# A Mamba-2 mixer with an FFN on one core: the state update as three passes of split operands, and one buffer for gated values

## What is computed

```python
proj = x @ in_proj_w.T                       # gate 8192 | hs 8192, B 1024, C 1024 | dt 128
hBC = silu(causal_conv4(proj[hs, B, C]))     # 4 taps per channel
xch = hs * dt                                # per head (128 heads of 64, 8 groups of B and C with 128 states)
# chunks of 128 tokens, 4 in a batch, A_cum = cumsum(dt * A) inside a chunk
Y_diag = (C @ B.T * exp(segsum)) @ xch
states = einsum('lhn,hl,lhp->hpn', B, exp(A_cum[-1] - A_cum), xch)   # what a chunk adds to the state
state  = state * exp(A_cum[-1]) + states                             # carried to the next chunk
Y_off  = (C @ state) * exp(A_cum)
g = (Y_diag + Y_off + hs * D) * silu(gate)
out = rmsnorm_per_group(g) * norm_w @ out_proj_w.T
x = layernorm(x + out);  x = layernorm(x + x @ W.T + bias + lora(x))
```

## Time and profile before

| | |
|---|---|
| median of 3 runs | 1648.08 us (1647.91 to 1648.45) |
| the profiled execution's own time | 1651.37 us |
| its span in the profile | 1648.4 us |
| PE busy | 1614.3 us, 98% of the span |
| DVE, ACT, POOL busy | 1348.8 us, 1221.5 us, 1021.2 us |
| granted TensorE clock, mean | 0.996 of 2.4 GHz |
| DMA | 178.65 MB, 33.7% of 16 engines on the main queue |

### The profile page before, as it was taken

One profiled execution on the slowest core, in us unless ns is written; L12 is line 12 of the kernel. 1 busy time (PEld: TensorE's weight loads), 2 busy tenths in 40 slices (PEclk: granted clock), 3 DMA queues, 4 the chain that ended last, 5 costly groups with the idle time before them and its releaser, 6 DMA issues. The chain is left out here.

```text
span 1648.4 us, 26983 instructions
## 1 busy us (share of the span) xinstructions
PE 1614.3 (98%) x9072; PEld 1292.7 (78%) x9072; DVE 1348.8 (82%) x1855; ACT 1221.5 (74%) x2373; POOL 1021.2 (62%) x829
## 2 busy tenths in 40 slices
PE   7999999999999999999999999999999999999898
PEld 6777888778888788878887788887887878877655
DVE  5677798869987799877988689986998879887876
ACT  5868778776777877776787777788677778777742
POOL 4456667566675757656665656756566666666654
PEclk9999999999999999999999999999999999999999
DMA  3633324333242333423243333433323332333301
GB/s 125 238 110 103 113 84 157 88 103 103 84 158 84 113 96 107 132 91 113 92 123 118 99 100 94 145 97 113 99 100 120 103 119 94 108 110 102 128 27 45
DMA packets 87144, 178.65 MB, mean 108 GB/s; under 512 B 16480, under 2 KB 20576, under 8 KB 86624
## 3 DMA queue, kind: packets, MB, share of 16 engines
q1 hardware_dynamic: 83760, 175.72, 33.7%
q10 hardware_dynamic: 3248, 1.22, 0.3%
HBM read 172.17 MB, written 4.72 MB: 107 GB/s over the span
## 5 line engine op out<-in xcount | busy, mean ns | idle before, releaser
L952 POOL TENSOR_TENSOR w_lo<-raw,w_hi 128x512 fp32r<-128x512 f32 x209 | 297.9, 1426 | 295.5 <-ACT w_hi L709 294.5
L495 PE MATMUL proj<-x_hi,w_hi 128*128 128x512 f32 x1160 | 462.8, 399 | 8.5 <-DVE x_lo L1216 6.9
L496 PE MATMUL proj<-x_lo,w_hi 128*128 128x512 f32 x1160 | 452.9, 390 | 0.0
L497 PE MATMUL proj<-x_hi,w_lo 128*128 128x512 f32 x1160 | 452.8, 390 | 0.0
L1103 DVE SCALAR_TENSOR_TENSOR hs<-proj,uch,hs 128x511 f32<-128x511 f32 (+2 forms) x384 | 285.4, 744 | 56.9 <-ACT hs L736 51.6
L791 ACT ACTIVATE decay<-decay,tok 128x128 f32<-128x128 f32 x1024 | 312.5, 392 | 0.0
L1004 POOL TENSOR_TENSOR dh<-dh,eac 128x512 f32<-128x512 f32 x96 | 127.8, 1331 | 228.5 <-DVE eac L1151 228.4
L495 PEld LDWEIGHTS proj<-x_hi,w_hi 128*128 128x128 f32 x1160 | 218.9, 189 | 50.8 <-issue 6.9
L1125 DVE TENSOR_TENSOR decay<-decay,cb 128x1024 f32<-128x1024 f32 x128 | 190.9, 1491 | 80.2 <-ACT decay L797 77.7
L497 PEld LDWEIGHTS proj<-x_hi,w_lo 128*128 128x128 f32 x1160 | 218.3, 188 | 46.0
L496 PEld LDWEIGHTS proj<-x_lo,w_hi 128*128 128x128 f32 x1160 | 219.0, 189 | 41.6
(11 more groups left out here) (121 smaller groups left out, 2765.7 us busy)
## 6 DMA issues: line engine op xcount, KB each, us to landing
decay<-acum_d SPq DMA_DIRECT2D x128, 512.0 KB, 4.0
raw<-w_t SPq DMA_DIRECT2D x209, 256.0 KB, 2.8
eac<-eacum_d SPq DMA_DIRECT2D x192, 128.0 KB, 4.1
wo_raw<-wo_t SPq DMA_DIRECT2D x32, 256.0 KB, 3.6
c_new<-wo_t SPq DMA_DIRECT2D x32, 256.0 KB, 4.8
hs<-x_t SPq DMA_DIRECT2D x8, 256.0 KB, 5.3
acc<-x_tok SPq DMA_DIRECT2D x1, 2048.0 KB, 8.6
out<-acc SPq DMA_DIRECT2D x8, 256.0 KB, 2.0
```

The costliest lines, as they stand in the source:

```text
L495: nc.tensor.matmul(dst[:], w_hi[:, ws, k, :], x_hi[:, k, cols], start=(k == 0), stop=False)
L496: nc.tensor.matmul(dst[:], w_hi[:, ws, k, :], x_lo[:, k, cols], start=False, stop=False)
L497: mm = nc.tensor.matmul(dst[:], w_lo[:, ws, k, :], x_hi[:, k, cols], start=False, stop=(k == KC - 1))
L952: nc.gpsimd.tensor_tensor(w_lo[:, s].rearrange("p a b -> p (a b)"), raw[:, s, :], w_hi[:, s].rearrange("p a b -> p (a b)").bitcast(F32), A ...
```

## The change

Four things move together.

1. The state update becomes three F32R matmuls, b_hi·xd_hi, b_hi·xd_lo and b_lo·xd_hi. B in token order is stored as `b_hi` and `b_lo` for the six chunks of a group that update a state (VectorE: one copy and one subtraction in the place of one copy; for chunks 3 and 7 no transpose and no copy at all). GpSimd makes `xd`, then casts it to `xd_hi` and subtracts to `xd_lo`, with a wait for its own result between them.
2. On TensorE the update comes behind `front` instead of ahead of it. VectorE's `front` therefore waits for `xd_scaled`, GpSimd's last reading of `xdt`.
3. `g_hi` and `g_lo` have one buffer. `g_hi` waits for `out_ready` of the step before (`s`, not `s - 1`). ScalarE makes the square first and `g_hi` after it; VectorE makes `g_lo` after the sums of squares and the layer norms' statistics.
4. `eac` has one buffer; its load waits for `dh_ready` of the step before its use and stands first in the step's list on SyncE.

```diff
 def load_eac(q, g, e, c):
-            slot = (carried(0, e, c) - 1) % 2
-            wait(q, dh_ready, step(g, e, c) - 1)
+            wait(q, dh_ready, step(g, e, c))
...
                         mm.then_inc(yd_ready, 1)
+                        off, ne, ncn = after(e, c)
+                        if not (last and off):
+                            front(g + off, ne, ncn)
                         if c % CPB != CPB - 1:
                             pe.wait_ge(xd_ready, updates(g, e, c))
                             wait(pe, yoff_scaled, carried(g, e, c))
-                            nc.tensor.matmul(p_st[:], b_tok[:, c, :], xd[:].rearrange("p a b -> p (a b)"),
-                                             start=True, stop=True).then_inc(st_ready, 1)
-                        off, ne, ncn = after(e, c)
-                        if not (last and off):
-                            front(g + off, ne, ncn)
+                            xh, xl = xd_hi[:].rearrange("p a b -> p (a b)"), xd_lo[:].rearrange("p a b -> p (a b)")
+                            nc.tensor.matmul(p_st[:], b_hi[:, bslot(c), :], xh, start=True, stop=False)
+                            nc.tensor.matmul(p_st[:], b_hi[:, bslot(c), :], xl, start=False, stop=False)
+                            nc.tensor.matmul(p_st[:], b_lo[:, bslot(c), :], xh, start=False, stop=True).then_inc(st_ready, 1)
...
                         act.wait_ge(gated, s + 1)
-                        wait(act, out_ready, s - 1)
-                        nc.scalar.activation(g_hi[:, c % 2].rearrange("p a b -> p (a b)"), y[:].rearrange("p a b -> p (a b)"),
-                                             ACT.Copy).then_inc(ghi_ready, 1)
                         wait(act, sqs_ready, s)
                         nc.scalar.activation(ysq[:], y[:], ACT.Square).then_inc(sq_ready, 1)
+                        wait(act, out_ready, s)
+                        nc.scalar.activation(g_hi[:].rearrange("p a b -> p (a b)"), y[:].rearrange("p a b -> p (a b)"),
+                                             ACT.Copy).then_inc(ghi_ready, 1)
...
-                nc.gpsimd.tensor_tensor(xd[:], xdt[:], bcast(tok[:, e, 2, c, :], 2, HD), ALU.mult).then_inc(xd_ready, 1)
+                n = updates(g, e, c)
+                nc.gpsimd.tensor_tensor(xd[:], xdt[:], bcast(tok[:, e, 2, c, :], 2, HD), ALU.mult).then_inc(xd_scaled, 1)
+                pool.wait_ge(xd_scaled, n)
+                nc.gpsimd.tensor_copy(xd_hi[:], xd[:]).then_inc(xdhi_ready, 1)
+                pool.wait_ge(xdhi_ready, n)
+                nc.gpsimd.tensor_tensor(xd_lo[:], xd[:], xd_hi[:].bitcast(F32), ALU.subtract).then_inc(xd_ready, 1)
...
                 dve.wait_ge(hid_ready, step(g, e, c) + 1)
+                wait(dve, xd_scaled, carried(g, e, c))
                 nc.vector.tensor_tensor(xdt[:], p_hid[:], bcast(tok[:, e, 1, c, :], 2, HD), ALU.mult).then_inc(xdt_ready, 1)
...
-                        dve.wait_ge(ghi_ready, s + 1)
-                        nc.vector.tensor_tensor(g_lo[:, c % 2].rearrange("p a b -> p (a b)"), y[:].rearrange("p a b -> p (a b)"),
-                                                g_hi[:, c % 2].rearrange("p a b -> p (a b)").bitcast(F32), ALU.subtract).then_inc(glo_ready, 1)
-                        if c < 7 and (c + 1) % CPB and len(STEP_TILES[e][c]) == 1:
-                            scale_off(g, e, c + 1)
                         for ln in lns:
                             ln_stats_1(*ln)
                         dve.wait_ge(sq_ready, s + 1)
...
                         for ln in lns:
                             ln_stats_3(*ln)
+                        dve.wait_ge(ghi_ready, s + 1)
+                        nc.vector.tensor_tensor(g_lo[:].rearrange("p a b -> p (a b)"), y[:].rearrange("p a b -> p (a b)"),
+                                                g_hi[:].rearrange("p a b -> p (a b)").bitcast(F32), ALU.subtract).then_inc(glo_ready, 1)
+                        if c < 7 and (c + 1) % CPB and len(STEP_TILES[e][c]) == 1:
+                            scale_off(g, e, c + 1)
```

More of the change, by code:

```diff
@@ L131, in mixer_ffn_kernel @@
         ysq = sb("ysq", [P, UT, P])
-        g_hi, g_lo = sb("g_hi", [P, 2, UT, P], F32R), sb("g_lo", [P, 2, UT, P], F32R)
+        g_hi, g_lo = sb("g_hi", [P, UT, P], F32R), sb("g_lo", [P, UT, P], F32R)
         state = sb("state", [P, UH, HD])
@@ L449, in body @@
                     for c in range(8):
+                        o1, e1, c1 = ahead(e, c, 1)
+                        if c1 % CPB and not (last and o1):
+                            load_eac(sp, g + o1, e1, c1)
                         od, ed, cd = ahead(e, c, 2 if c % 2 else 4)
@@ L452, in body @@
                             load_decay(sp, g + od, ed, cd)
-                        o2, e2, c2 = ahead(e, c, 2)
-                        if c2 % CPB and not (last and o2):
-                            load_eac(sp, g + o2, e2, c2)
                         for t in tiles_of(e, c, last):
```

47 lines of the change are left out of this document (28 added, 19 removed).

## The result

The changed kernel takes 1665.51 us (median of 4 runs, 1662.74 to 1666.32), the kernel before 1648.22 (4 runs, 1647.91 to 1648.45): a ratio of 1.0102, with a 95% interval of 1.0085 to 1.012. That is 17.3 us slower, where 4.7 were forecast and the range ended at 1664. The profiled execution took 1662.74 us, its span 1660.9.

What follows compares the result with a forecast made beforehand. TensorE alone was taken to set the time up to about 1550 us; −21.8 + 2.5 + 3.4 + 6.4 + 13.7 + 2.5 − 2 = +4.7 us on the 1648.08 median gave 1652.8 us, range 1642 to 1664.

Steps and rivals of the forecast that it cites:

- the price of GpSimd's contention: GpSimd's new cast and subtraction slow VectorE: +6.4 us in (0, 1) and +2.5 us in (1, 4).
- +6.4 us for (0, 1): Step (0, 1): new GpSimd work slows one g_lo in VectorE's unbroken run, 0.8 us in each of 8 groups.
- +2.5 for (1, 4): Step (1, 4): TensorE waits 0.35 us for the state in seven groups; bounds 0 to 7 us.
- GpSimd's work blocking VectorE whole: Rival: each new operation costs 2.0 us, not 0.8, in (0, 1); +9.6 us, 1662.4 us; chance 0.18.
- grown to 1.4: Sign in the profile: the wait ahead of project_out in (0, 1) grows from 0.2 to about 1.4 us.
- a rival of 0.07 behind tile C: Rival: the clock falls at each wait for tile C, 3.1 us seven times; +22 us, 1675 us; chance 0.07.
- the last unit's term: Last unit: earlier statistics save 5.8 us, waits at lora_down cost 3.9; net −2 us, bounds −6 to +6.
- The update and the transposes, −21.8: TensorE: shorter updates save 20.2 us and 16 dropped transposes of B 1.6 us; bounds −18 to −25.
- Gains lost ahead of hs, +2.5: Step (0, 7): transposes wait for ScalarE's silus, so 0.31 us of savings is lost in each of 8 groups.
- Lost ahead of `wo_lo`, +3.4: Step (0, 1): project_out waits for VectorE's wo_lo, so 0.42 us of savings is lost in each of 8 groups.
- Tile C, +13.7: Step (1, 1): g_hi's one buffer delays tile C's weight split; TensorE waits 1.95 us in seven groups.
- `eac`, 0: The one-buffer load of eac takes 4 us, needed a step of 11 us later; cost nothing.

Runs made afterwards that it cites:

- e3: Changed kernel without GpSimd's cast and subtraction: the low part of the scaled tokens left out, xd_hi read twice, three matmuls kept; 1649.69 us.
- e2: Changed kernel with the three matmuls of the state update ahead of front again, all else kept; 1666.19 us.
- e1: Changed kernel with ScalarE's splits and drains of the further tiles at c = 1 ahead of the wait for project_out and g_hi; 1653.59 us.
- e8: Kernel before with only the one buffer for the gated values and the new ScalarE and VectorE order that comes with it; 1664.9 us.
- e4: Kernel before with GpSimd's extra work alone, a copy of xd in place and its product a second time, values unchanged; 1663.91 us.
- e11: Changed kernel with add_normed of the previous group's last two chunks moved on VectorE from (0,0) and (0,1) to (0,2) and (0,3); 1662.61 us.
- e7: Changed kernel with the edits of e3 and e1 together; 1637.19 us, 0.9912 of the kernel before.

## Why the prediction was wrong in size

**The failed step is the price of GpSimd's contention**, together with what its wait does to the clock. The sum has +6.4 us for (0, 1), "one `g_lo` doubled", from bounds of nothing to 2.0 a group, and +2.5 for (1, 4): 8.9 us in all. By e3 GpSimd's new work costs 15.8 us. Of these, 11.6 stand in the steps (195.60 a group against 193.94 in e3, seven times): 10.3 in (0, 0) and (0, 1), for the 6.4, and 1.7 in (1, 4), for the 2.5 (the other steps give 0.3 back). The other 4 are no step's length at the full clock. Three things were off in the 6.4.
- *How much.* Not one instruction was slowed in VectorE's run ahead of (0, 1) but two, `add_normed` and `g_lo`, by 0.79 us each, and against e3 the pair of `wo_lo` by 0.8 more. `var` is 1.95 us later than in e3, near the term's bound of 2.0, which the prediction left to a rival. That rival, GpSimd's work blocking VectorE whole, came out at 1662.4, 3 us under the result. The rows show such blocks from end to end: `xd_lo` takes its usual 1.29 us and ends at 1060.38, and `g_lo`, begun inside it, ends at 1060.93, 0.55 us later, whereas alone it takes 0.68; `xd` ends at 1057.99 and `add_normed` at 1058.54, again 0.55 later. In the traces of both kernels this holds for all 152 cases in which GpSimd had 0.3 us or more left of such an operation when one of these two began: they end 0.54 to 0.56 us behind it. The Trainium skill ("SBUF — State Buffer", Who interferes with whom) calls the shared pair of ports an exclusive lock; the trace agrees.
- *Where.* It was put at project_out, which showed a wait of 0.20 us, and that wait "grown to 1.4" was to be the proof. It went away. The product C·B, which stands 3.4 us ahead of project_out in (0, 1) of the kernel before, waits for `var`; it had 0.06 us of cover, and no row of the waits shows a cover.
- *What moved toward it.* The prediction counted front ahead of the update as moving the update 0.4 us back, and not as moving C·B 0.9 us forward, past what VectorE owes it. e2 shows that this alone decides nothing, since the update then waits in its place, but it is why the wait was at L522.

**The clock was put at nothing**, or at a rival of 0.07 behind tile C; it did not fall behind tile C's waits in any trace. In the profiled run it fell behind two of the waits for `var`. A window of the changed kernel around one of them, columns as above, and rows of TensorE in it:

```profile
1258.00:1266.00 8.00, 6.20 (x36) 4.93 (x32) 6.35 (x8) 4.99 (x13) 6.85 (x6) 0.79 0.67 226
```

```profile
1261.18 0.57 PE L522 MATMUL p_misc<-cT,bT 128*128 128x128 f32 x2 [1.80 <-DVE var L1156]
...
1262.61 0.63 PE L671 MATMUL p_st<-xd_hi,b_lo 128*128 128x512 f32 x1
1263.04 0.63 PE L499 MATMUL proj<-x_hi,w_hi 128*128 128x512 f32 x1
```

The matmuls start 0.43 us apart and not 0.23, the clock's lower level of 1.2 GHz, until 1264.75; such a group takes 197.2 us in place of 195.6. Without the two falls the profiled run would have been 9.3 us above the profiled run of before, with them it is 12.5. e1, which keeps the waits for `var`, shows the same: two falls, each behind one of its seven, and means of 0.992 to 0.995. Behind the seven waits of 1.35 us in e2, of 1.7 us for `w_lo` in e8 and of 0.95 us in e4 there is none. And e2 and e11, whose groups take 0.7 and some 0.4 us longer than those of the changed kernel, are as fast and 3 us faster: 4 to 6 us each that no step shows. What made the clock fall behind four waits of 1.8 us and not behind the other ten of the two traces stays open, and e3 has a mean of 0.993 in one run without any of them.

**What put the time outside the range.** Without the last unit's term the sum makes +6.7 us, and the steps show +8.9 (below); the last unit was to bring 2 and lost 0.8. That is 9.7 us in place of 4.7, a time of 1657.9, inside the range. The other 7.6 of the 17.3 us are in no step at the full clock: 3.2 are the two falls of the profiled run. The rest, some 4 us, lies in executions that left no trace; their means, 0.993 and 0.994 against 0.995 in the profiled one, speak for more such falls, and that is argued, not shown.

**What held, term by term.**
- The update and the transposes, −21.8: PE's busy time fell by 21.6 in e7. The steps with an update are 0.22 to 0.24 us shorter. (The distance from Y_diag to project_out is 2.21 us and not the 2.13 announced: 0.09 of the gain lies behind project_out's start, in its first matmul.)
- Gains lost ahead of hs, +2.5: 8.5 − 5.8 = 2.7. Lost ahead of `wo_lo`, +3.4: in e7, where this wait stands alone, 7.9 − 4.8 = 3.1.
- Tile C, +13.7 (1.95 a group): 12.2 (1.74), and 11.9 by e1. e8 gives 14.7 for the whole of the third part of the change, the last unit with it. This is the one large term that held in place, cause and size.
- (1, 4), +2.5: the step is 0.24 us longer than in e3, 1.7 in seven groups. `eac`, 0: no wait for its load.
- The last unit, −2: the stretch from its second Y_diag to the end is 111.8 us against 112.0, of which the updates are 1.1; so it lost 0.8. The 6.73 us row is gone, and five waits at `lora_down`, 6.2 us in all, where the sum had three and 3.9, took its place.

By group this closes: before 194.07; update −1.80 (e7), buffer +1.67 (e3 less e7), GpSimd's work +1.66 (after less e3), after 195.6. The first is had in eight groups, the other two are paid in seven: −14.4 + 11.7 + 11.6 = +8.9 us.

## What to carry to other kernels

Where one engine is busy 98% of the time, list for each step what it will need from the others and when that is ready, covers of a tenth of a microsecond included; a list of waits names only those already spent, and a change that makes a feeder late and the consumer early is paid at the thinnest cover. Work given to an idle engine is not free when it slows a busy one: price it on the longest unbroken run of the slowed engine, with every instruction in it that can be hit. And wait for an operand at the instruction that reads it: one wait for four operands ahead of the first cost 7.6 us in the kernel before, half of it in the first group.

## What the runs showed of the hardware

- VectorE and GpSimd block each other whole. `add_normed` and `g_lo`, when begun inside a GpSimd operation that reads SBUF, ended 0.55 us behind its end (alone they take 0.74 and 0.68), so a late start cost up to 1.0 us. It goes both ways: GpSimd's cast took 0.61 us alone, 0.95 in 44 of the 96 updates and 1.5 to 1.6 in 34, ending 0.47 us behind the VectorE instruction that it met; the prediction took 0.61 throughout. The Trainium skill ("SBUF — State Buffer", Who interferes with whom) has a VectorE instruction with two inputs in SBUF contend with a GpSimd one that reads SBUF. The trace agrees with it for these two, both of whose large operands are in SBUF.
- The granted clock fell to its lower level behind waits of 1.8 us in an engine that was busy 96% of the time, in two of seven groups of the changed kernel and two of seven in e1, and cost 1.6 us each time, nearly as much as the wait itself. Behind waits of 1.7 us elsewhere in the program it did not fall.
- Three F32R matmuls of 128 x 128 x 512 took 0.22 us less than one in plain float32 (0.77 against 0.90 us to the next start, and 0.09 in the matmul behind them).
